# Two-layer transformer kernel: side work of the first layer's front and of the second layer's last chunks as entries of the attention's tables

## The reference

```
layernorm(x) = (x - mean) / sqrt(var + 1e-5)                      # over the 256
# sublayer 1, latent attention, 16 heads of 16, causal
c_q  = ln(x @ W_d_q.T + b_d_q) * q_g + q_b                        # 85 wide
c_kv = x @ W_d_kv.T + b_d_kv                                      # 128 + 8
kv_n = ln(c_kv[:, :128]) * kv_g + kv_b
q    = c_q @ W_u_q.T + b_u_q          # per head 8 plain, 8 rotated (angle: head index)
k_n, v = split(kv_n @ W_u_kv.T + b_u_kv)                          # per head 8 and 16
k    = [k_n, rotary(c_kv[:, 128:])]   # the rotated 8 shared by the heads
y    = softmax(mask(q @ k.T / 4)) @ v ;  f = y @ W_o.T + b_o
# sublayers 2 and 4, feed-forward, int8 weights, 256 -> 1024 -> 256
f = ((silu(x @ Wg * s_g) * (x @ Wu * s_u)) @ Wd) * s_d
# sublayer 3, plain causal attention, 16 heads of 16: qkv = x @ W.T + b
```

## Time and profile before

| | us |
|---|---|
| median of 3 runs | 1224.86 (1224.44 to 1225.69) |
| profiled execution | 1224.29 |
| its span | 1222.5 |
| PE busy | 1138.8 (93%) |
| DVE busy | 1025.0 (84%) |
| ACT busy | 781.2 (64%) |
| POOL busy | 341.4 (28%) |
| mean granted clock of PE | 0.969 |

### The profile page before, as it was taken

One profiled execution on the slowest core, in us unless ns is written; L12 is line 12 of the kernel. 1 busy time (PEld: TensorE's weight loads), 2 busy tenths in 40 slices (PEclk: granted clock), 3 DMA queues, 4 the chain that ended last, 5 costly groups with the idle time before them and its releaser, 6 DMA issues.

```text
span 1222.5 us, 36826 instructions
## 1 busy us (share of the span) xinstructions
PE 1138.8 (93%) x14888; PEld 583.7 (48%) x14888; DVE 1025.0 (84%) x2714; ACT 781.2 (64%) x1565; POOL 341.4 (28%) x579
## 2 busy tenths in 40 slices
PE   4768999999999999899997889999999999999996
PEld 3532335444444444665654333444544454465664
DVE  6859999999998784777775799999999978648776
ACT  2452677887888988344442546788888898944332
POOL 5232211122201224434442221111221112434443
PEclk9986999999999999999997799999999999999998
DMA  5273100211200000001123430021120000000001
GB/s 181 78 218 95 52 14 6 67 29 31 53 3 3 3 3 3 4 32 34 46 78 105 104 94 16 16 64 25 34 58 3 3 3 3 4 2 1 18 18 35
DMA packets 31610, 50.03 MB, mean 41 GB/s; under 512 B 7245, under 2 KB 24143, under 8 KB 31431
## 3 DMA queue, kind: packets, MB, share of 16 engines
q1 hardware_dynamic: 25376, 41.95, 12.3%
q0 software_dynamic: 5488, 5.34, 1.5%
q10 hardware_dynamic: 576, 0.39, 0.1%
HBM read 32.56 MB, written 14.68 MB: 39 GB/s over the span
## 4 chain that ended last, share of the span: by engine, by line
PE 69%; DVE 22%; ACT 2%; DMA 2%; issue 2%; POOL 2%; ACTq 0%; POOLq 0%; DVEq 0%
PE ps L1049 66%; DVE m_tile L913 7%; DVE ps L915 3%; PE ps L1224 1%; DVE region_p L793 1%; DVE stats L756 1%; DMA q_stack<-m_rows 1%; DVE region_p L967 1%; DVE k_stack L999 1%; PE ps L1044 1%; DVE k_stack L996 1%; DVE region_p L769 1%; DMA q_parts<-parts 1%; DVE region_p L987 1%; DMA causal<-in_causal 1%
## 5 line engine op out<-in xcount | busy, mean ns | idle before, releaser
L684 ACT ACTIVATE region_p<-ps 128x512 f32<-128x512 f32 (+3 forms) x1280 | 592.7, 539 | 158.7 <-PE ps L1049 153.3
L913 DVE TENSOR_REDUCE m_tile<-ps 128x1 f32<-128x512 f32 x768 | 496.9, 684 | 25.2 <-PE ps L1049 22.3
L1049 PE MATMUL ps<-k_stack,q_stack 96*32 96x512 bf16 (+3 forms) x5120 | 405.7, 360 | 20.2 <-DMA k_stack<-in_ones 7.4
L1049 PE MATMUL ps<-q_stack,k_stack 99*32 99x512 bf16 (+3 forms) x5120 | 402.5, 350 | 6.3 <-DMA q_stack<-m_rows 3.1
L1049 PE MATMUL ps<-region_p,v_all 128*17 128x512 f32 (+3 forms) x2560 | 292.7, 531 | 0.0
L915 DVE CUSTOM_DVE_ANT_0 ps<-ps,causal 128x128 f32<-128x128 f32 (+3 forms) x512 | 247.4, 498 | 25.6 <-PE ps L1049 23.8
L1049 PEld LDWEIGHTS ps<-k_stack,q_stack 96*32 96x32 bf16 x5120 | 143.1, 97 | 204.1 <-DVE m_tile L913 66.7
L1049 PEld LDWEIGHTS ps<-q_stack,k_stack 99*32 99x32 bf16 x5120 | 141.0, 96 | 185.9 <-ACT region_p L684 97.0
L563 POOL TENSOR_SCALAR_AFFINE_SELECT region_p<-region_p 128x512 f32<-128x512 f32 x128 | 81.3, 635 | 240.0 <-ACT region_p L684 237.3
L1049 PE MATMUL ps<-region_a,w_ffn 128*128 128x512 f16 x512 | 123.7, 387 | 6.0 <-DVE region_a L801 6.0
L718 ACT ACTIVATE k_stack<-ps,cols 128x512 f32<-128x512 f32 x64 | 44.0, 688 | 107.3 <-PE ps L1049 102.3
(11 more groups left out here) (112 smaller groups left out, 885.1 us busy)
## 6 DMA issues: line engine op xcount, KB each, us to landing
k_parts<-parts SPq DMA_DIRECT2D x16, 384.0 KB, 2.8
q_parts<-parts SPq DMA_DIRECT2D x16, 384.0 KB, 3.6
q_stack<-q_parts SPq DMA_DIRECT2D x32, 192.0 KB
k_stack<-k_parts SPq DMA_DIRECT2D x32, 192.0 KB
q_stack<-q_parts SPq DMA_DIRECT2D x32, 128.0 KB
k_stack<-k_parts SPq DMA_DIRECT2D x32, 128.0 KB
X<-in_x SPq DMA_DIRECT2D x4, 512.0 KB, 6.8
q_stack<-q_parts SPq DMA_DIRECT2D x32, 64.0 KB
```

Of the source, the lines that this page charges most:

```text
L684: nc.scalar.activation(probs[:, o.j % SLOTS, o.h, o.off:CH], psT[:, o.k % TBANKS, o.off:CH], ACT.Exp, scale=SCALE).then_inc(s.exp_done, 1)
L913: nc.vector.tensor_reduce(maximum, scores, AX.X, ALU.max).then_inc(s.ring_free, 1)
L1049: return pe.matmul(o, a, b, start=first, stop=last)
```

## The change

The first layer's front stands in the table of the first attention, and the last two chunks' work of the second attention in a table of its own (TURNS_1). New letters: g statistics of a chunk of x and n its norm, x a pair's transposes, d the down projection of a pair, q square root and z norm of a latent chunk, i and j the transposes of its q and kv halves, u, r, m a unit's product, remainder and mid/low part, v and w a value pair and its evacuation; b and e in the second table are the last chunk's branch norm and norm. All that need a bank (x u v d i j) share the four ring banks with S, M and Y, and the release of a bank is now that of whatever entry stood there (ring_release). The core of the diff (the tables are cut to their first line, waits renamed from ring to seq numbers are left out):

```diff
 TURNS = (
-    "SSSSSSSSSSSSSSSSSSSSMSSSSSSSSSSSSSSSTTSSSTTTSSSSTTTSSTSSVSSSTSSSTSTSSTTMSTTSVSSSSSSVSSSVSSTSSTSS"
+    "ggnnxxgxurxddqmzddqzijjuungxrmrimurumrurmxddmquvzrnSwSSSiSSSmSSSuSrxSSSSSvmSwSSSSjSMSSSxSSSSSSuS"
+    "rmddquzTrSSSTSSSSTiSSmTTSTSSSuSTTrSTVTSSSjSSSSMVTSTSSuSrTTSvwTSTmSmSvSwSTTSVSTSSTSTSuSrSTuTSvrwS"
...
+TURNS_1 = (
+    "SSSuSrSSSSmSSSSSSSSbuMvrwurSSemuSrvwSTSSSTTSSSTSxmSSSSTTSSTSSSSSTSxSSSSSmVSSTTSTSSTSuSSrVTSmSMTS"
...
+IN_BANKS = "SMYxuvdij"
...
+    NU, VU, EARLY, EARLY_V = 16, NT // 2, 8, 4
...
-        c_down = region_p[:, 0:NT * (DQ + DKV)].rearrange("p (i c) -> p i c", i=NT)
+        c_down = ffn_flat[:, 0:NT * (DQ + DKV)].rearrange("p (i c) -> p i c", i=NT)
+        x_hat = w_ffn[:].bitcast(F32).rearrange("p (b i c) -> p b i c", b=3, i=TPC)
...
-                return u // 3 - 2 if u % 3 == 0 and u >= 6 else None
-            return u // 4 if u % 4 == 3 else None
+                return u // 3 if u < 12 and u % 3 == 2 else None
+            return u // 4 if u % 4 == (3 if u < EARLY else 1) else None
...
+        def ring_release(L, o):
+            if o.kind == "X":
+                return turn[2 * L].moved_a, o.k + 1
+            if o.kind == "U":
+                return proj[L].rem, o.k + 1
+            if o.kind == "V":
+                return proj[L].v_sb, o.k + 1
+            if o.kind == "DOWN":
+                return proj[0].z, 2 * TPC * (o.k // 2 + 1)
+            if o.kind == "QT":
+                return proj[0].zq_sb, o.k + 1
+            if o.kind == "KVT":
+                return proj[0].zkv_sb, o.k + 1
+            return s.ring_free, L * RING_N + o.seq + 1
...
+                        if L == 1 and c == NCH - 1:
+                            sp.wait_ge(ffn[0].down, NCH * NI)
+                            sp.wait_ge(s.t_filled, T_N + 1)
+                            for c1 in range(NCH):
+                                load_stacks(1, c1)
...
-            load_ffn(0)
-            load_ones(1)
-            split_bias(0)
-            split_bias(1)
+            split_row(bd_parts, row("b_down"), proj[0].b_down)
+            rotate_queries()
+            split_row(bv_parts, row("b_v", 0), proj[0].b_v)
+            split_row(bo_parts[:, 0, :, :], row("b_o", 0), oproj[0].bias)
+            split_row(bo_parts[:, 1, :, :], row("b_o", 1), oproj[1].bias)
...
+                    if o.kind == "DNORM":
+                        act.wait_ge(proj[0].rstd, 2 * o.k + 2)
+                        for i in range(TPC * o.k, TPC * (o.k + 1)):
+                            for w, half in HALVES:
+                                nc.scalar.activation(c_down[:, i, half], down_half(i, half), ACT.Identity,
+                                                     scale=rstd[:, i, w:w + 1], bias=shift[:, i, w:w + 1]
+                                                     ).then_inc(proj[0].z, 1)
+                    if o.kind == "VALUE" and L == 0:
+                        act.wait_ge(proj[0].v_ps, o.k + 1)
+                        nc.scalar.copy(v_all[:, 2 * o.k:2 * o.k + 2, :, 0:DH],
+                                       ps[:, v_bank(0, o.k), :].rearrange("p (t h d) -> p t h d", t=2, h=H)
+                                       ).then_inc(proj[0].v_sb, 1)
...
-                split_mid(L, NU - 1)
-                convert_ffn(L)
...
                         nc.scalar.copy(y_chunk[:, o.n % 2, :], ps[:, PV_BANK, :]).then_inc(s.y_evac, 1)
+                        if 5 <= o.n < 8:
+                            convert_ffn(L, (o.n - 5,))
...
+                    if o.kind == "BRANCH":
+                        normalize_branch(2, NCH - 1)
+                        add_last(2)
+                        stats_residual(2, NCH - 1)
+                    if o.kind == "DOWN":
+                        dve.wait_ge(p.down_ps, o.k + 1)
+                        for i in (2 * o.k, 2 * o.k + 1):
+                            for w, half in HALVES:
+                                nc.vector.bn_stats(stats[:, i, w, :], down_half(i, half)).then_inc(p.var, 1)
+                    if o.kind == "DNORM":
+                        bs = slice(TPC * o.k, TPC * (o.k + 1))
+                        dve.wait_ge(p.std, o.k + 1)
+                        nc.vector.reciprocal(rstd[:, bs, :], std[:, bs, :]).then_inc(p.rstd, 1)
+                        dve.wait_ge(p.rstd, 2 * o.k + 1)
+                        nc.vector.scalar_tensor_tensor(shift[:, bs, :], mv[:, bs, :, 0], -1.0, rstd[:, bs, :], ALU.mult,
+                                                       ALU.mult).then_inc(p.rstd, 1)
...
-                    pe.wait_ge(p.rem, NU)
-                    pe.wait_ge(p.v_sb, VU)
+                    mm(ps[:, bank, 0:2 * (DQ + DKV)], pick[0:96, :], bd_parts[0:96].rearrange("p t c -> p (t c)"), True, False)
+                for o in ORDERS[L]:
+                    if L == 1 and o.ring in (1, 2):
+                        pe.wait_ge(f.evac, NT - TPC + 2 * o.ring)
                     if o.ring is not None and o.ring >= RING:
-                        pe.wait_ge(s.ring_free, L * RING_N + o.ring - RING + 1)
+                        pe.wait_ge(*ring_release(L, IN_RING[L][o.ring - RING]))
```

More of the change, by code:

```diff
@@ L102, in plan_attention @@
+SIDE_TURNS = {"x": "X", "u": "U", "v": "V", "b": "BRANCH", "e": "XHAT", "r": "REM", "w": "VALUE", "m": "MID",
+              "g": "XSTATS", "n": "XNORM", "d": "DOWN", "q": "DSTD", "z": "DNORM", "i": "QT", "j": "KVT"}
+IN_BANKS = "SMYxuvdij"
+Step = namedtuple("Step", "kind n g Q h r c kt off first last hp ring k j sel seq", defaults=(None,) * 16)
+def plan_attention(turns, early_pairs, early_units, early_values):
     steps = STEP_ORDER
@@ L142, in build_program @@
 def build_program(nc, D, out):
-    STEPS, ORDER = plan_attention()
+    NU, VU, EARLY, EARLY_V = 16, NT // 2, 8, 4
+    STEPS, ORDER = plan_attention(TURNS, 0, 0, 0)
+    ORDERS = (ORDER, plan_attention(TURNS_1, NT // 2 - 2, EARLY, EARLY_V)[1])
     NSTEP = len(STEPS)
-    RING_N = sum(1 for o in ORDER if o.ring is not None)
+    RING_N = sum(1 for o in ORDER if o.seq is not None)
     T_N = sum(1 for o in ORDER if o.kind == "T")
@@ L755, in stats_of @@
                         dve.wait_ge(ready, i + 1)
-                    nc.vector.bn_stats(stats[:, i, which, :], tiles[:, i, :]).then_inc(after, 1)
+                    nc.vector.bn_stats(stats[:, i, which, :], tiles(i)).then_inc(after, 1)
                 for i in batch:
@@ L924, in _ @@
                     if o.kind == "MT":
[L925 removed]
+                        dve.wait_ge(s.ring_filled, base + o.seq + 1)
                         if o.n >= 2:
@@ new lines, in latent_transposes @@
+                def latent_transposes(kind, c, half, done):
+                    pe.wait_ge(proj[0].z, 2 * TPC * (c + 1))
+                    for t in range(TPC):
+                        ins = pe.transpose(z_bank(kind, c)[0:half.stop - half.start, t * P:(t + 1) * P],
+                                           c_down[:, TPC * c + t, half], ident[:])
+                    ins.then_inc(done, 1)
+                if L == 1:
+                    pe.wait_ge(turn[2].moved_a, 6)
+                    pe.wait_ge(p.rem, EARLY)
+                    pe.wait_ge(p.v_sb, EARLY_V)
```

494 lines of the change are left out of this document (227 added, 267 removed).

## The result

| | before | changed |
|---|---|---|
| median (us) | 1224.86 | 1228.70 |
| all runs (us) | 1223.53 to 1225.69 | 1227.39 to 1235.74 |
| profiled execution, its span | 1224.29, 1222.5 | 1232.8, 1230.7 |
| ratio to before | | 1.0046, 95% interval 1.0028 to 1.0065 |

The profiled execution of the changed kernel lies 4 us above its median. Kernels with the same front differ by up to 2.7 us in when the first score starts (56.4 to 59.2 us in five profiles), so the work of each stretch is compared, not the clock time of one event. The forecast was 1201 us, with 1184 to 1216 as its range.

A forecast was written before the change was run, and what follows sets the result against it. Bound by a sum of places where PE or DVE waits or sets the pace, not one engine's load. Span 1222.5 - 16.4 (layer 0) - 7.5 (layer 1) = 1198.6, as a median 1201 us; range 1184 to 1216.

The forecast's parts named there:

- What bounds the kernel: Whole kernel: PE and DVE take turns in the front, DVE paces to the 97th score, PE to the output projection.
- six stack loads 3.4 to issue, 2.8 for the last to land: Layer 0, end of the chain to the first score: loads of the first stack, in us, reaching 48.5.
- the time of the banks: Layer 0: first two scores need banks of down pairs 4 and 5, free about 50; first score taken at 50.0.
- Carrying 350.3 us over: Layer 0, neg_max over 48 to output projection: the 350.27 us before carried over, with side work left behind added.
- Stacks late: Rival, chance 0.13: layer 0's stacks 1 to 3 arrive late, three waits of 3 to 4 us, 1211 us.
- A stretch of over 355 us: Sign: a PE-paced stretch longer than 355 us would be the casts and prove a step wrong.
- Casts, 0.5 us each: Three weight casts a layer behind the y copies of steps 5 to 7: 0.5 us each, bounds 0 and 1.89.
- Ring waits, 8 us in layer 0: First score to 97th: side entries hold score banks, 8 us beyond DVE's added work, bounds 0 and 32.
- the 5 us of ring waits: Layer two up to its 97th score: 5 us for PE's twelve side entries, bounds 0 and 17.
- Layer two's PE-paced stretch: After layer two's 97th score: 350.54 carried over, plus unit 15 and values 7 (3.6), two T (0.4), casts 1.5.
- The feed-forward's end: Units 8 to 11 and values 4 and 5 leave it: layer two's first maximum at 648.5 us against 665.23.
- Low clock: Rival, chance 0.02: clock stays at 0.50 up to the 97th scores, over 1270 us; slower than before from near 0.63.

The follow-up runs named there:

- front_first: Changed kernel with all side entries of the first layer's table ahead of the first score, in their old order: 1239.7 us, ratio 1.0124.
- before_late: Kernel before, with layer 0's loads of group 1's stacks waiting for 56 T products instead of 1: 1235.96 us in one run.
- keys_early: Changed kernel with layer 0's four key loads of head group 1 queued ahead of the stores of units 12 to 15: 1221.2 us, ratio 0.9979.
- single_runs: Changed kernel with each stack load of three or two copies cut into loads of one copy (16 rows): 1210.6 us, ratio 0.9884.
- hold_group2: keys_early with group 2's stack loads queued only after the first T of step 3 (layer 0) or step 4 (layer 1): 1218.0 us, 0.9946.
- combo_pool_casts: hold_group2 (built on keys_early), plus DVE normalizing each latent chunk's second pair and the weight casts in pieces on POOL: 1208.0 us, ratio 0.9873.
- best_single: combo_pool_casts with stack loads cut into loads of one copy, as in single_runs: 1197.1 us, ratio 0.9786.
- warm_clock: keys_early with eight extra PE products in the wait for the first stack, adding nothing to the output: 1223.9 us.

## Why the prediction was wrong

- **What bounds the kernel** held: up to the neg_max over 48 DVE sets the pace, and front_first shows the overlap worth 16.4 us. DVE was busy 61.2 us there, where the forecast's terms add up to 58.7 (50.3 before and 8.4 added).
- **"six stack loads 3.4 to issue, 2.8 for the last to land"** failed: the last load needed 7.8 us, not 2.8. I took the landing of a store of 128 rows for loads of 48, 32 and 16, whose own landing no row gave, and never set 768 KB against a rate. That is 5.0 us. The chain before it is the other part: the low parts ended at 43.2 instead of 39, with PE at half clock from 34 to 40 us and z at 0.345 instead of 0.28 us each. The chain ended at 58.5 instead of 48.5; the miss is 8.5 since the forecast took 50.0, the time of the banks.
- **Carrying 350.3 us over** failed, and weighs most: 14.2 us. I counted the instructions left behind the 97th score, but not the DMAs. The store of unit 15 moved past the start of group 1's loads; they began at 144 instead of 102 us, with 26 us to their use where 33 are needed. "Stacks late" was among the rivals, but for group 0's stacks only and at 10 us. before_late, keys_early and single_runs show it from three sides. In the profiles this stretch of layer 0 falls from 367.1 to 361.1 us with keys_early, to 356.5 with hold_group2 and to 354.5 in combo_pool_casts, against 352.9 forecast. A stretch of over 355 us was named as a sign of the casts; the casts were the smallest of the three.
- **The m rows** (maxima, 3 KB each), which the forecast never prices, landed late beside those loads. With group 2's loads held back the two intervals fell by 4.6 and 1.8 us.
- **Casts, 0.5 us each**, was mis-sized: ACT's time cost 1.5 and 3.7 us net in two intervals, 1.2 to 1.8 us a cast in others; 3 forecast, 4.5 measured over both layers by moving them to POOL.
- **Ring waits, 8 us in layer 0**: the 52.3 us carried over hold 2.1 us of waits, so 10.1 were forecast in all; DVE stood idle 13.8 of 75.0 us there. single_runs alone leaves 10.7, combo_pool_casts 10.2, best_single 5.6, so late stacks and z share the rest, and no run separates them fully. In layer two 7.1 were forecast and 2.1 came: none of the 5 us of ring waits, which is the miss of -4.6.
- **Layer two's PE-paced stretch**, 362.4 against 356.0: it is 360.6 in keys_early (whose edit doesn't touch layer two, so this is spread in the landing of the rows), 358.9 in hold_group2 and 355.8 in combo_pool_casts. So rows of maxima and casts explain it, in about equal parts.
- **The feed-forward's end** was right within 1.3 us. **Low clock** as a rival of over 1270 us was not seen, and its threshold was not reached: the mean clock up to the neg_max over 48 was 0.78 and 0.97, where before had 0.77 and 0.81. So the denser table did leave the low clock sooner in layer two, and hardly in layer 0.
- The interval behind the ninth maximum of layer 0 is still 3.3 us longer than before with no cast on ACT (42.0 against 38.7). PE is busy 1.1 us more there, with eight more products in the interval, and waits 1.5 us for a mask of POOL and 0.7 us on "issue". Which of the order of the table and POOL's work makes these waits stays open; with the casts early on ACT instead of on POOL it was 41.3.

## What to carry to other kernels

When work moves later in a table, write down for each of its DMAs what it releases and when that is needed, and compare the bytes with a rate read from the trace, not with the landing time of another transfer. A DMA share that stood at 2/16 or 3/16 while an engine waited was a problem of shape here: look at the outermost dimension of the loads, and put 16 rows there, before changing any order. A stretch is carried over only if its inputs arrive as early as before.

## What the runs showed of the hardware

With loads of three and two copies of 16 rows the engines moved 78 GB/s at a share of 0.19 and 49 at 0.13 while PE waited; the same bytes in loads of one copy, 64 KB each, landed in 2.3 us a load (median of single_runs). Transfers of 3 KB took 1.6 to 1.7 us with no such load on its way (before, at 176 to 178 us) and up to 5.9 beside loads. A clock raised to 1.00 by extra products was 0.74 behind the next 16 scores (warm_clock); in best_single it was 0.50 in those 16 and 0.96 behind them. A cast of 128x2048 from int8 to bf16 took 1.90 us on ACT, one of 128x512 0.62 us on ACT and on POOL.
